# Reordering the attention pipeline's step: where the value matmuls and the score matmuls stand among the transposes

## The reference

```python
# B, S, E, H = 4, 1024, 512, 16; D = E // H = 32
Q, K, V = heads(layernorm(x), Wq, bq), heads(ctx, Wk, bk), heads(ctx, Wv, bv)
scores = einsum('bhqd,bhkd->bhqk', Q, K) / sqrt(D) + adj[None, None]
scores = where(mask == 0, -inf, scores)
out = einsum('bhqk,bhkd->bhqd', softmax(scores), V)         # then heads merged, @ Wo.T + bo
x = x + tanh(g_xattn) * out
# feed-forward: h = layernorm(x); a global gate from mean(h); three cycles of
# h = h + coupling(h) * twist(h), coupling a small four-layer net with GELU
x = x + tanh(g_ffn) * ffn(layernorm(x))
```

## Time and profile before

| | |
|---|---|
| median of three runs | 1736.85 us (1735.43 to 1736.92) |
| the profiled execution, its own time | 1736.92 us |
| its span in the profile | 1735.1 us |
| attention phase in it | about 290 to 1243 us |
| PE busy | 1708.5 us (98%) |
| DVE busy | 1443.4 us (83%) |
| ACT busy | 1244.5 us (72%) |
| granted TensorE clock | full in the attention phase |

### The profile page before, as it was taken

The page is one execution under the profiler, slowest core; times in us unless marked ns, Lnnn a source line. Parts: engine busy times, 40 slices in busy tenths (PEclk is TensorE's granted clock), DMA queues, the critical chain, the costliest instruction groups (busy, mean ns, idle before and its releaser), DMA issues. The chain is left out here.

```text
span 1735.1 us, 34186 instructions
## 1 busy us (share of the span) xinstructions
PE 1708.5 (98%) x12456; PEld 1291.2 (74%) x12456; DVE 1443.4 (83%) x2554; ACT 1244.5 (72%) x2185; POOL 659.9 (38%) x590
## 2 busy tenths in 40 slices
PE   9999999999999999999999999999999999999997
PEld 7887888777777777777777777777775685774863
DVE  6554555999999999999999999999678976868868
ACT  4222223999999999999999999999574365365455
POOL 3432341423278542586432885633235010100100
PEclk9999999999999999999999999999999999999999
DMA  7778675865468665567764686455403513221101
GB/s 279 274 239 289 225 270 158 189 184 135 131 160 198 129 154 123 135 212 142 160 154 116 185 182 138 120 111 153 162 17 98 169 40 119 88 74 49 64 1 49
DMA packets 152472, 254.65 MB, mean 147 GB/s; under 512 B 17024, under 2 KB 69504, under 8 KB 152320
## 3 DMA queue, kind: packets, MB, share of 16 engines
q1 hardware_dynamic: 101936, 158.78, 28.7%
q0 software_dynamic: 49808, 92.82, 23.8%
q10 hardware_dynamic: 576, 1.05, 0.2%
HBM read 168.44 MB, written 84.15 MB: 146 GB/s over the span
## 5 line engine op out<-in xcount | busy, mean ns | idle before, releaser
L1021 DVE CUSTOM_DVE_ANT_0 a_neg<-a_sc_ps,am 128x1024 f32<-128x1024 f32 x512 | 621.5, 1214 | 1.4 <-PE a_sc_ps L853 1.3
L961 ACT ACTIVATE a_prob<-a_neg,a_row_min 128x1024 f32<-128x1024 f32 x512 | 585.5, 1144 | 13.9 <-DVE a_row_min L1021 7.8
L867 PEld LDWEIGHTS a_tr_ps<-ident,a_prob 128*128 128x128 f32 x4096 | 461.0, 140 | 89.2 <-issue 53.2
L867 PE MATMUL a_tr_ps<-ident,a_prob 128*128 128x128 f32 x4096 | 519.8, 274 | 0.9 <-ACT a_probT L939 0.9
L996 DVE COPY a_probT<-a_tr_ps 128x512 f32<-128x512 f32 x512 | 350.5, 685 | 36.8 <-PE a_tr_ps L867 35.3
L939 ACT ACTIVATE a_probT<-a_tr_ps 128x512 f32<-128x512 f32 x512 | 304.0, 594 | 35.2 <-PE a_tr_ps L867 16.2
L749 POOL DMA_DIRECT2D a_q_st<-q_parts x144 | 79.4, 558 | 201.2 <-PE a_sc_ps L853 165.4
L853 PE MATMUL a_sc_ps<-k_first,a_q_st 96*128 96x512 f32 x384 | 126.3, 427 | 0.1
L853 PE MATMUL a_sc_ps<-a_k_st,a_q_st 96*128 96x512 f32 x384 | 125.8, 426 | 0.0
L887 PE MATMUL a_o_ps<-a_probT,a_v 128*32 128x256 f32 x2048 | 123.6, 382 | 0.6 <-ACT a_o L950 0.6
L887 PE MATMUL a_o_ps<-a_probT,v_first 128*32 128x256 f32 x2048 | 123.8, 382 | 0.0
(11 more groups left out here) (227 smaller groups left out, 3166.2 us busy)
## 6 DMA issues: line engine op xcount, KB each, us to landing
a_q_st<-q_parts POOLq DMA_DIRECT2D x144, 128.0 KB, 3.9
k_first<-k_parts POOLq DMA_DIRECT2D x24, 512.0 KB, 8.3
a_k_st<-k_parts POOLq DMA_DIRECT2D x24, 512.0 KB, 8.1
a_m_raw<-mask SPq DMA_DIRECT2D x24, 512.0 KB, 5.0
a_adj_raw<-adj SPq DMA_DIRECT2D x24, 512.0 KB, 5.9
k_parts<-p_out_hi SPq DMA_DIRECT2D x32, 256.0 KB, 4.2
k_parts<-p_out_lo SPq DMA_DIRECT2D x32, 256.0 KB, 6.2
v_all<-p_v_out SPq DMA_DIRECT2D x8, 1024.0 KB, 4.4
```

The source lines that it names most:

```text
L867: last = pe.transpose(tr_ps[:, bank(u, half), j * P:(j + 1) * P], prob[:, r % NPROB, t * P:(t + 1) * P], ident[:])
L961: act.activation(prob[:, r % NPROB, :], neg[:, r % 2, :], ACT.Exp, scale=-1.0, bias=row_min[:, r % 2:r % 2 + 1], accum_out=row_sum[:, r // ...
L1021: dve.tensor_tensor_reduce(out=neg[:, r % 2, :], in0=sc_ps[:, r % 2, :], in1=am[:, 2 * qb + qt, :], scale=-1.0, scalar=3.4e38, op0=ALU.add ...
```

## The change

The three `step` functions are rewritten; each engine still does the same instructions for the same units, and no buffer, wait or transfer is changed. On PE `weighted_values` moves from between S2 and T8 to behind the T8 of the last unit (`r + 3`), at the step's end, and the `scores` calls move by one unit against the transposes. The transpose of the inverse sums moves from the end of the group's second step to the third step. ACT's output copy comes one unit later in the block, its reading of the last unit's transposes is in the same step, and two exponentials stand in a row at another place. DVE has two readings in a row and two `negated` in a row, and its copy of the inverse sums moves from the third to the fourth step. The diff has first PE's step, then ACT's `weights` and its step, then DVE's step.

```diff
             def step(p, r):
+                scores(*shifted(p, r, 3))
                 transposes(p, r, 0)
-                scores(*shifted(p, r, 3))
-                scores(*shifted(p, r, 4))
                 transposes(p, r, 1)
                 transposes(p, r + 1, 0)
+                scores(*shifted(p, r, 4))
+                scores(*shifted(p, r, 5))
                 transposes(p, r + 1, 1)
-                scores(*shifted(p, r, 5))
-                for n in range(QUAD):
-                    weighted_values(p, r + n)
                 transposes(p, r + 2, 0)
                 transposes(p, r + 2, 1)
+                if r % UG == UB:
+                    transpose_rinv(2 * p + r // UG, isinstance(p, int) and p == 0 and r < UG)
                 scores(*shifted(p, r, 6))
                 transposes(p, r + 3, 0)
                 transposes(p, r + 3, 1)
-                if r % UG == QUAD:
-                    transpose_rinv(2 * p + r // UG, isinstance(p, int) and p == 0 and r < UG)
+                for n in range(QUAD):
+                    weighted_values(p, r + n)
...
-                if r % UB == 0:
+                if r % UB == 1:
                     read_output(blk - 2, (r // UB) % 2, isinstance(p, int) and p == 0 and r // UB < 2)
...
             def step(p, r):
                 weights(p, r + 1)
-                read_transposes(*shifted(p, r, -1))
+                weights(p, r + 2)
                 read_transposes(p, r)
-                weights(p, r + 2)
                 read_transposes(p, r + 1)
                 weights(p, r + 3)
+                read_transposes(p, r + 2)
                 weights(*shifted(p, r, 4))
-                read_transposes(p, r + 2)
+                read_transposes(p, r + 3)
...
-            read_transposes(NPAIR - 1, PAIR - 1)
...
             def step(p, r):
-                for n in range(QUAD):
-                    negated(p, r + n)
-                    read_transposes(*shifted(p, r, n - 3))
-                    if r % UG == UB and n == 2:
-                        read_rinv(2 * p + r // UG, isinstance(p, int) and p == 0 and r < UG, o_ps[0:UG, QB:QB + P])
+                negated(p, r)
+                read_transposes(*shifted(p, r, -3))
+                read_transposes(*shifted(p, r, -2))
+                if r % UG == UB + QUAD:
+                    read_rinv(2 * p + r // UG, isinstance(p, int) and p == 0 and r < UG, o_ps[0:UG, QB:QB + P])
+                negated(p, r + 1)
+                negated(p, r + 2)
+                read_transposes(*shifted(p, r, -1))
+                negated(p, r + 3)
+                read_transposes(p, r)
```

## The result

The changed kernel takes 1754.92 us (median of four runs, 1753.62 to 1756.28) against 1736.42 us of the kernel before in the same measurement: a ratio of 1.0107, 95% interval 1.0090 to 1.0125. It is 18.5 us slower. I had said 5.3 us slower, in a range up to +10: the direction was right, the size was not, and the time lies above the range.

What follows compares the result with a forecast made beforehand. PE's own instruction list was taken as the bound; +6.2 us for new neighbours, -1.0 for score-run losses and +0.3 for the last step made +5.5, stated as 1742.2 us, range 1735.5 to 1747.

Steps and rivals of the forecast that it cites:

- That PE's own list bounds the kernel before: Regular steps: PE never waits, and the step of 7.35 us is the sum of PE's own distances.
- That the pauses around W32 are PE's own price and no waits: Idle loads, 0.36 us ahead of W32 and 0.41 behind: PE's cost of changing between 128-column and 32-column weights.
- The new neighbours: PE's step: three distances summing to 3.34 us are replaced by three summing to 3.39; +0.05 per step, +6.2 us.
- No change: Rival: loads behind W32 cost the same whatever stands there, or the widths' change covers them; 1737 us, chance 0.20.
- ACT, DVE and the inverse sums, at nothing: Reordered ACT and DVE lists and the moved inverse-sums transpose: same work, DVE's pause only moves, PE hides it; 0 us.
- Clearly slower: Rival: S4's third load waits for the negated fed by the S2 behind W32; 0.17 per step, 1763 us, chance 0.11.
- The credit of 1.0 us for small losses in score runs: PE's score runs: S4's third load no longer late for DVE's min pass; a third of 3.1 us won, -1.0 us.
- the structural term: PE's own distances around the moved W32: 0.05 us more per step, 6.2 us over 125 steps.
- The last step: End of the attention phase: T8 and the final W64 wait, one weight-width change each way is saved; +0.3 us.

Runs made afterwards that it cites:

- before_recip: Kernel before plus a DVE reciprocal of 128x32 behind the fourth negated pass of every step; 1737.52 us, ratio 1.0007.
- before_shorter: Kernel before with all four negated passes of a step over 896 of the 1024 keys; 1735.45 us, ratio 1.0001.
- w_split: Kernel before with W32 in two halves, one moved between S4 and T12, the other left in place; 1791.24 us, ratio 1.0316.
- after_shorter: Changed kernel with all four negated passes of a step over 896 of the 1024 keys; 1742.48 us, ratio 1.0043.
- after_short_first: Changed kernel with only every fourth negated pass (unit r) over 960 of the 1024 keys; 1749.47 us, ratio 1.0072.
- after_short_rest: Changed kernel with the three other negated passes of each step (units r+1 to r+3) over 960 of the 1024 keys; 1756.05 us, ratio 1.0116.
- after_recip: Changed kernel plus a DVE reciprocal of 128x32 behind the fourth negated pass of every step; 1774.71 us, ratio 1.0217.

## Why the prediction came out as it did

**That PE's own list bounds the kernel before: right.** DVE's work could be lengthened (before_recip) or cut by 0.53 us per step (before_shorter), and the time stayed.

**That the pauses around W32 are PE's own price and no waits: right.** In the changed kernel the one behind is 0.41 as before; w_split has each pause twice. That the width of the weights is what costs it, and not another property in which W32's matmuls differ, was not tried apart. The Trainium skill's rule on the change of tiling mode, that it drains TensorE ("TensorEngine Tiling (Array Packing)", Key Properties), agrees with both traces. It gives no price; in w_split one more change in and out costs 0.29 us of PE's time, the exposed loads included.

**The new neighbours, +0.05 us per step or 6.2 us: the size is right, the reason given for it is not.** W32 to S2 was forecast at 1.89 and is 1.86 to 1.87, S2 to T12 0.53 and is 0.57, T8 to W32 0.97 and is 0.97 where T8 isn't late. The first two miss in opposite directions and nearly cancel; that is luck. after_shorter against before_shorter, in which no wait for DVE makes PE's matmuls late, gives 1742.48 - 1735.45 = 7.0 us. But the 0.05 does not come from a longer exposed load behind W32: W32 to its successor is the same 1.86 to 1.87 with T8 there before and with S2 there after. Behind it a pair of scores loses 0.02 (S2 to T12 0.57 against 0.55), and transposes lose more, 0.06 (T12 to S2 1.29 behind the half in w_split against 1.23). The cost is on the way in. A pair of scores needs 0.64 to W32 where it needs 0.55 to transposes, 0.09 more. T8 needs 0.97 where eight transposes ahead of scores would take 1.23 - 4 x 0.11 = 0.79 (my estimate from T12), 0.18 more. Together 0.09 more ahead of W32 and 0.04 less behind it.

The rival *No change* is out by this 7.0 us, which stays when the wait is gone. It was joined to the rule that equal columns mean equal loads (the Trainium skill, "TensorE: Matmul & The Clock Gate", LDWEIGHTS (loading the stationary operand)). The loads take 190 and 140 ns here, against that rule, but by the distances above their length is not what makes the 0.05.

**"ACT, DVE and the inverse sums, at nothing": wrong, and this is the step that failed.** I wrote of DVE's pause that it "has to be somewhere" and that PE hides it. I had followed DVE's lateness to one reader, the third load of S4, and priced that as the rival *Clearly slower*. That load does wait for its `negated`, 0.06 behind its end in each step, but it makes nothing late: S4 to T12 is 1.01. But DVE's list has another reader, T8's half 0, which waits for the reading of the unit two before. Moving W32 from between S4 and that half 0 to behind it took 1.86 us out of the slack of this chain, and it was left with 2.83 us of chain against 2.79 of PE in the step shown, and 2.87 in the mean. S2 to T8 grows by the difference, from 0.55 to 0.63, and T8 to W32 from 0.97 to 0.99, together 0.105 per plain step. In the 15 steps with the transpose of the inverse sums neither grows.

The phase adds up so. From the first W32 on, 124 steps took 7.388 us each before and take 7.536 now, 18.4 us more. Of these the neighbours are 6.4 us (3.404 for the three distances in place of 3.352, in all 124) and T8's wait 109 x 0.105 = 11.4; about 0.6 are left, from S2's wait for the same `negated` (T12 to S2 is 1.24 in place of 1.23) less the 0.5 of the next paragraph. The start and the end of the phase together make 0.7, and 19.0 came. after_short_first, after_short_rest, after_recip and after_shorter show the wait from both sides, and the 15 steps show it in the changed kernel itself.

**The credit of 1.0 us for small losses in score runs: not there** in a size that counts. S4 to T12 went from a mean of 1.016 to 1.012, 0.5 us.

**The rival *Clearly slower*** had the right kind of mechanism and the wrong reader, at 21 us beside the structural term where 12 came. It got 0.11 of the chance; a walk with every wait of PE's list would have shown that its place was T8, and that the margin there was near zero.

**The last step, +0.3 us:** 0.7 by the traces, start and end taken together, since W32 now comes later in its step: from the first score load to the first W32 it is 2.4 us more (23.4 against 21.1), and behind the last regular step 1.7 us less (12.6 against 14.3).

No version came out of this that beats the kernel before. Its order has the least costly neighbours of W32 that were tried, and its list is what binds it.

## What to carry to other kernels

When a long run on the bounding engine is moved, list each wait that now has the run no longer between its producer and its consumer, and walk each of them, not only the one that comes to mind. An idle engine's share (DVE had 0.3 us in each step) says nothing about a chain that goes through it once: what counts is the time from what starts it to what needs it. Where a pause of the bounding engine is put down to different engines at the same length, suspect that it is the engine's own, as here, and put one more of it into the list to see. And read a pause of the weight loads and the time that it costs PE apart: the shorter pause ahead of W32 here goes with the larger cost.

## What the runs showed of the hardware

A change of PE from 128-column to 32-column weights leaves the loads idle for 0.36 us behind scores and 0.17 behind transposes, and the change back for 0.41 us ahead of either. By the starts of its matmuls the change in costs PE 0.09 us behind scores and about 0.18 (an estimate, from T12's 1.23) behind transposes, and the change back 0.02 ahead of a pair of scores and 0.06 ahead of a run of transposes, beside what lies within W32's 1.86. A DVE memset of 128x64 (0.11 us by its record) between a `negated` and a PSUM reading moved the following instruction by at most some hundredths of a us, and a reciprocal of 128x32 with a record of 0.35 by 0.15 to 0.19: the length of a short record is not what it costs in a list. Where the loads stood idle some 0.3 us ahead of the first one, a run of eight transposes takes 0.99 to the next W32, where they stood idle 0.19 it takes 0.97.
